# The rotary swap by transfers, two groups of query products instead of three, and the product with the values for two units in every second round

## The chip, the cores and the metric

The kernel runs on one core of a Trainium2 chip. The metric is the device time of one execution in microseconds; three runs of the kernel before were timed, and their median stands below. TensorE (PE) does the matmuls, and its weight loads are PEld. VectorE is DVE, ScalarE is ACT, GpSimd is POOL, and SyncE (SP) issues transfers.

## What is computed

The reference is one transformer block with modulated layer norms: latent attention over S = 2048 tokens with 16 heads, and then a mixture of 8 experts. The change lies in the attention:

```python
q = _rms_norm(x @ w_qa, q_a_norm_w) @ w_qb            # 96 -> 16 heads x (128 + 64)
q_nope, q_rope = (q[..., :D_NOPE], q[..., D_NOPE:])
...
x1 = x[..., ::2]                                      # _rotate_half
x2 = x[..., 1::2]
return jnp.stack((-x2, x1), axis=-1).reshape(x.shape)
...
return x * cos + _rotate_half(x) * sin                # of 64 features
...
scores = jnp.einsum('bhsd,bhtd->bhst', q_full, k_full) * scale   # causal
attn = jax.nn.softmax(scores, axis=-1)
out = jnp.einsum('bhst,bhtd->bhsd', attn, v)
```

The kernel multiplies the key's up-projection into the query, so that scores are taken between 64 latent and 64 rotary features, 128 in all, and the values are the 64 latent features.

## The kernel before

It has three stages: `prepare` (weights, layer norm, latent keys and queries), `attend`, and `experts`. The change touches the first in how the query weights are laid out, and the second.

**Units.** A pair is one head pair and one group g of 512 query tokens (PAIRS, line 54). There are 32 pairs, in the order g = 3, 1, 2, 0 within a head pair (0, 1, 2, 3 in the first). An item is one head of a pair, and a unit (line 61) is 256 keys against the 512 queries of an item: 2g full units, and two on the diagonal, of which the second needs only the last 256 queries. There are 320 units. Every item has an even number of them, so the short diagonal unit always has an odd number.

**Rounds.** All engines run through the same rounds r (line 80), each in its own order. In round r TensorE does the scores of unit r, with up to three chunks of the search for row maxima put between and behind the halves, then perhaps the broadcast of an item's shift (`shift_rows`), then perhaps one group of query products, and then the product with the values of unit r-2 (`weigh`):

```python
if part < 3:
    query_products(p, part)
if r >= 2:
    weigh(r - 2)
```

A score is three matmuls of rounded parts (high with high, high with low, low with high), upon a bank that ScalarE or VectorE has seeded with the shift. ScalarE takes the exponential of unit r and seeds the bank of unit r+2. GpSimd subtracts the 16-bit high part of the exponentials (`low_parts`, lines 664 to 676), and both parts go into the product with the values. The tiles pt and pt_lo are rings of four units.

**The query of a pair** is prepared in rounds that begin with PREP_ROUND (line 79), six rounds or more before its first chunk. Pairs 7, 11, 15, 19, 23 and 27, with g = 0, are prepared four rounds before the next pair, as pair 0 is before pair 1; else the distance is 7 to 18. From pair 2 on PREP_ROUND is even. Each of three groups of products is three matmuls of 512 columns into one of three work banks: group 0 gives head 0 (latent and rotary features), group 1 head 1, and group 2 the rotary features of both with even and odd swapped and signed. VectorE multiplies groups 0 and 1 by the cosine into qf (line 757), ScalarE copies the latent half (692), and VectorE multiplies group 2 by the sine in its bank (760) and adds it (770). Then ScalarE rounds qf to q_hi (699) and GpSimd subtracts to q_lo (661). There is one buffer qf: the next pair's first VectorE and ScalarE operations wait until q_lo of this pair is written.

**The work banks** are handed out in order by WORK_ORDER (lines 98 to 103) to chunks, shifts and query groups alike; use n waits until use n-3 has been seen by its readers (`wait_seen`).

**SyncE** loads the weights of a head pair (lines 640 to 642) once the last group of the pair before is done, and per pair four transfers of cosine and sine into turn_by (648), which has room for two pairs.

## Time and profile before

| | us |
|---|---|
| three runs | 1254.86, 1255.21, 1247.85 |
| median | 1254.86 |
| the profiled execution | 1254.86 |
| its span | 1253.1 |
| busy in the span: PE | 1146.3 (91%) |
| PEld | 958.8 (77%) |
| DVE | 846.8 (68%) |
| ACT | 787.5 (63%) |
| POOL | 690.3 (55%) |

The page gives the span in 40 slices of 31 us, each digit being tenths of a slice:

```profile
PE   2856899999999999999999999999999778989897
DVE  2632876677676776777777677776675576767676
ACT  1254577777777878777787787877777532322222
POOL 0022366777777768686787776877777711202000
PEclk9876699999999999999999999999999879989998
```

The attention is the stretch of nines. A matmul's record holds its way through the array, and the records of successive matmuls overlap; how often one starts is read from the start times in the view in order of time. Averages over the whole span mix the three stages.

### The profile page before, as it was taken

What the parts mean: (1) busy time and instruction counts of PE and PEld (TensorE: products, weight loads), DVE (VectorE), ACT (ScalarE), POOL (GpSimd) and SP (SyncE); (2) the same over time, 40 slices, a digit from 0 to 9 for tenths busy, and PEclk for the clock granted to TensorE, in tenths of its full rate; (3) what the DMA queues carried; (4) which work ended last, traced back from release to release, by engine and by line L of the source; (5) the groups of instructions that cost most, each with busy time, mean ns of one, the idle gap of its engine ahead of it and who ended that gap; (6) DMA issues with size and microseconds to landing.
All of it is one profiled execution on the core that took longest, in us unless ns stands there. A gap on an engine that the chain in (4) does not pass through costs nothing. (4 is left out here: it accounts for less than half of the span.)

```text
span 1253.1 us, 27841 instructions
## 1 busy us (share of the span) xinstructions
PE 1146.3 (91%) x11372; PEld 958.8 (77%) x11372; DVE 846.8 (68%) x1900; ACT 787.5 (63%) x1166; POOL 690.3 (55%) x569
## 2 busy tenths in 40 slices
PE   2856899999999999999999999999999778989897
PEld 1744577888888888888888888888887667888886
DVE  2632876677676776777777677776675576767676
ACT  1254577777777878777787787877777532322222
POOL 0022366777777768686787776877777711202000
PEclk9876699999999999999999999999999879989998
DMA  9301110000100200100020020010000310000000
GB/s 277 95 1 48 29 44 18 2 18 25 38 19 2 62 2 19 44 19 19 2 62 18 2 61 2 19 44 19 18 2 1 114 57 1 1 18 1 18 18 17
DMA packets 57695, 39.91 MB, mean 32 GB/s; under 512 B 7744, under 2 KB 57152, under 8 KB 57408
## 3 DMA queue, kind: packets, MB, share of 16 engines
q1 hardware_dynamic: 51216, 33.94, 9.2%
q10 hardware_dynamic: 6352, 4.19, 1.4%
q8 instruction: 90, 1.47, 0.5%
q14 instruction: 37, 0.30, 0.1%
HBM read 33.66 MB, written 4.46 MB: 30 GB/s over the span
## 5 line engine op out<-in xcount | busy, mean ns | idle before, releaser
L669 POOL TENSOR_TENSOR pt_lo<-pt 128x1024 f16<-128x1024 f32 x192 | 370.5, 1939 | 181.5 <-ACT pt L726 181.2
L782 DVE TENSOR_REDUCE gates<-bank 128x1 f32<-128x512 f32 x384 | 261.6, 689 | 148.0 <-PE bank L849 145.1
L717 ACT ACTIVATE pair<-shift 128x1024 f32<-128x1024 f32 x256 | 263.7, 1030 | 12.2 <-ACT pt L730 0.4
L726 ACT ACTIVATE pt<-pair 128x1024 f32<-128x1024 f32 x192 | 196.2, 1022 | 108.3 <-PE pair L876 107.7
L891 PEld LDWEIGHTS bank<-values,pt 128*128 128x128 bf16 x2176 | 196.8, 98 | 80.1 <-issue 52.6
L891 PE MATMUL bank<-values,pt 128*128 128x65 f16 x2176 | 235.2, 194 | 6.0 <-DVE lat L808 5.1
L893 PE MATMUL bank<-values,pt 128*128 128x64 f16 x2176 | 231.8, 192 | 0.0
L895 PE MATMUL bank<-values,pt_lo 128*128 128x65 f16 x2176 | 230.8, 194 | 0.0
L675 POOL TENSOR_TENSOR pt_lo<-pt 128x512 f16<-128x512 f32 (+3 forms) x256 | 178.3, 722 | 45.0 <-ACT pt L730 44.9
L893 PEld LDWEIGHTS bank<-values,pt 128*128 128x128 bf16 x2176 | 202.0, 98 | 0.0
L895 PEld LDWEIGHTS bank<-values,pt_lo 128*128 128x128 f16 x2176 | 201.3, 97 | 0.0
L779 DVE CUSTOM_DVE_ANT_0 bank<-bank,mask 128x128 f32<-128x128 f32 (+3 forms) x256 | 126.1, 498 | 53.8 <-PE bank L849 48.7
L730 ACT ACTIVATE pt<-pair 128x512 f32<-128x512 f32 (+3 forms) x256 | 110.4, 437 | 45.7 <-PE pair L876 32.1
L876 PE MATMUL pair<-q_hi,kt_a_hi 128*128 128x512 f32 (+1 forms) x320 | 131.1, 410 | 0.0
L876 PE MATMUL pair<-q_hi,kt_b_hi 128*128 128x512 f32 (+1 forms) x320 | 130.5, 408 | 0.0
L849 PE MATMUL bank<-kt_a_hi,q_hi 128*128 128x512 f32 (+2 forms) x320 | 118.6, 375 | 3.4 <-DVE qf L757 1.6
L849 PE MATMUL bank<-kt_b_hi,q_hi 128*128 128x512 f32 (+2 forms) x320 | 117.4, 369 | 0.7 <-DVE gates L779 0.6
L876 PE MATMUL pair<-q_lo,kt_a_hi 128*128 128x512 f32 (+1 forms) x320 | 117.2, 366 | 0.0
L876 PE MATMUL pair<-q_hi,kt_a_lo 128*128 128x512 f32 (+1 forms) x320 | 117.2, 366 | 0.0
L876 PE MATMUL pair<-q_hi,kt_b_lo 128*128 128x512 f32 (+1 forms) x320 | 117.1, 366 | 0.0
L876 PE MATMUL pair<-q_lo,kt_b_hi 128*128 128x512 f32 (+1 forms) x320 | 116.6, 364 | 0.0
L661 POOL TENSOR_TENSOR q_lo<-qf,q_hi 128x512 fp32r<-128x512 f32 x64 | 84.4, 1340 | 19.6 <-ACT q_hi L699 18.1
(218 smaller groups left out, 2380.0 us busy)
## 6 DMA issues: line engine op xcount, KB each, us to landing
turn_by<-rope_cos_by_feature SPq DMA_DIRECT2D x64, 128.0 KB, 3.0
turn_by<-rope_sin_by_feature SPq DMA_DIRECT2D x64, 128.0 KB, 3.0
xs<-in_L_attn_x ACTq DMA_DIRECT2D x1, 2048.0 KB, 25.5
lat<-in_L_attn_w_o SPq DMA_DIRECT2D x1, 2048.0 KB, 26.6
xs_again<-in_L_attn_x SPq DMA_DIRECT2D x1, 2048.0 KB, 8.1
out<-xs_again SPq DMA_DIRECT2D x4, 512.0 KB, 2.8
lat<-in_L_wmod SPq DMA_DIRECT2D x1, 1536.0 KB, 16.3
lat<-in_L_attn_w_qb SPq DMA_DIRECT2D x1, 1152.0 KB, 8.0
```

Of the source, the lines that this page charges most:

```text
L669: pool.tensor_tensor(out=pt_lo[:, at].rearrange("p a n -> p (a n)"), in0=full, in1=cut(full), op=ALU.subtract).then_inc(low_ok, 1)
L675: pool.tensor_tensor(out=pt_lo[:, at, half, live(u, half):], in0=full, in1=cut(full), op=ALU.subtract).then_inc(low_ok, 1)
L717: act.activation(s_pair[u % 2][:, :, :], shift[:, item % SHIFTS:item % SHIFTS + 1, :].to_broadcast([P, 2, BW]), ACT.Copy).then_inc(seeded[ ...
L726: act.activation(pt[:, at], s_pair[u % 2][:, :, :], ACT.Exp).then_inc(exp_done, 1)
L730: act.activation(pt[:, at, half, live(u, half):], s_pair[u % 2][:, half, live(u, half):], ACT.Exp).then_inc(exp_done, 1)
L779: dve.tensor_tensor_reduce(out=of, in0=of, in1=mask16[:, BW - n * P:], scale=1.0, scalar=LOWEST, op0=ALU.add, op1=ALU.max, accum_out=to).t ...
L782: dve.tensor_reduce(out=to, in_=of, axis=AXX, op=ALU.max).then_inc(work_seen["v"], 1)
L849: pe.matmul(work_of(w)[:, 0:cols], q, kt_hi[h][:, part * BW:part * BW + cols], start=True, stop=True).then_inc(work_done, 1)
L876: last = pe.matmul(to, keys[a], q[b], start=False, stop=(m == 2), skip_group_check=True)
L891: pe.matmul(to, cut(pt[:, at, half, mine]), with_one, start=(u == FIRST_UNIT[item] and half == 0 and t == 0), stop=False, skip_group_check ...
L893: pe.matmul(to[:, 0:KVL], cut(pt[:, at, half, mine]), low_values, start=False, stop=False, skip_group_check=True)
L895: last = pe.matmul(to, pt_lo[:, at, half, mine], with_one, start=False, stop=end, skip_group_check=True)
```

## The change

- In `prepare` the rotary columns of the query weights are laid out as evens and then odds (32 + 32), and the third block is no longer built; the keys' rotary features get the same order.
- A pair has two groups of products: group 0 gives the rotary features of both heads, group 1 the latent features of both.
- VectorE reads group 0 with three operations: by_sin = product x sign x sine, and the two products with the cosine into qf. Four transfers issued by SyncE then copy by_sin, its halves of 32 rows exchanged, into a new tile, swapped. Before a pair's four, SyncE issues the next pair's loads, with the tables in eight transfers instead of four.
- GpSimd adds swapped to qf in the third round of the preparation, after that round's low parts. ScalarE copies both latent halves in the second round. q_hi and q_lo come in the fourth round instead of the third.
- `weigh` is called for units r-3 and r-2 in odd rounds, and not in even ones.

```diff
-    WORK_ORDER += [("q", *PREP_AT[_r])] if _r in PREP_AT and PREP_AT[_r][1] < 3 else []
+    WORK_ORDER += [("q", *PREP_AT[_r])] if _r in PREP_AT and PREP_AT[_r][1] < 2 else []
 WORK = {w: n for n, w in enumerate(WORK_ORDER)}
 
 
 def seen_by(n):
 
     use = WORK_ORDER[n]
-    return {"max": "v", "shift": "a", "q": "va"}[use[0]] if use[0] != "q" or use[2] < 2 else ""
-
-
-SEEN = {e: [0, *itertools.accumulate(e in seen_by(n) for n in range(len(WORK_ORDER)))] for e in "av"}
+    return {"max": {"v": 1}, "shift": {"a": 1}, "q": {"v": 3} if use[-1] == 0 else {"a": 2}}[use[0]]
+
+
+SEEN = {e: [0, *itertools.accumulate(seen_by(n).get(e, 0) for n in range(len(WORK_ORDER)))] for e in "av"}
+
+
+def values_due(r):
+
+    return (r - 3, r - 2) if r >= 3 and r % 2 else ()
...
-                for at, e, of, sgn in moves:
-                    act.activation(pair_cols(wq_hi, at, e), of, ACT.Copy, scale=sgn).then_inc(wqh_ok, 1)
+                for at, of in moves:
+                    act.activation(half_cols(wq_hi, at), of, ACT.Copy).then_inc(wqh_ok, 1)
...
-                weights_of = None
-                weights_in = 0
-                for p, (hp, g) in enumerate(PAIRS):
-                    if hp != weights_of:
-                        weights_of, weights_in = hp, weights_in + 1
+                def loads(p):
+                    hp, g = PAIRS[p]
+                    if p == 0 or hp != PAIRS[p - 1][0]:
                         if p > 0:
-                            sp.wait_ge(work_done, WORK[("q", p - 1, 2)] + 1)
+                            sp.wait_ge(work_done, WORK[("q", p - 1, 1)] + 1)
                         for part in range(2):
                             sp.dma_start(wq[part][:, :].bitcast(F32), wq_dram[part, hp]).then_inc(wq_in, 16)
                     if p > 1:
-                        sp.wait_ge(q_sum, 2 * p - 2)
+                        wait_seen(sp, WORK[("q", p - 2, 0)])
                     for n, name in enumerate(("cos_t", "sin_t")):
-                        of = k[name].rearrange("d (j g p) -> d j g p", j=BT, g=NG)[:, :, g, :]
+                        of = k[name].rearrange("(i e) (j g p) -> e i j g p", e=2, j=BT, g=NG)[:, :, :, g, :]
                         for half in range(2):
-                            sp.dma_start(turn_by[half * DR:half * DR + DR, p % 2, n, :].rearrange("d (j p) -> d j p", j=BT),
-                                         of).then_inc(turn_in[p % 2], 16)
-                sp.wait_ge(wq_in, 32 * weights_in)
+                            for e in range(2):
+                                at = half * DR + e * (DR // 2)
+                                sp.dma_start(turn_by[at:at + DR // 2, p % 2, n, :].rearrange("d (j p) -> d j p", j=BT),
+                                             of[(e + n) % 2]).then_inc(turn_in[p % 2], 16)
+
+                def swap(p):
+                    wait_seen(sp, WORK[("q", p, 0)])
+                    if p > 0:
+                        sp.wait_ge(q_sum, 2 * p)
+                    for at in range(0, P, DR // 2):
+                        sp.dma_start(swapped[at:at + DR // 2, :], by_sin[at ^ (DR // 2):(at ^ (DR // 2)) + DR // 2, :]).then_inc(q_swapped, 16)
+
+                loads(0)
+                for p in range(len(PAIRS)):
+                    if p + 1 < len(PAIRS):
+                        loads(p + 1)
+                    swap(p)
+                sp.wait_ge(q_swapped, 64 * len(PAIRS))
+                sp.wait_ge(wq_in, 32 * NP)
                 for n in range(2):
-                    sp.wait_ge(turn_in[n], 64 * (len(PAIRS) // 2))
+                    sp.wait_ge(turn_in[n], 128 * (len(PAIRS) // 2))
 
             @block.gpsimd
             def _(pool):
                 pool.memset(ones_r[:, :].bitcast(F32), 1.0).then_inc(consts_ok, 1)
+
+                def query_sum(p, r):
+                    if r >= 0:
+                        pool.wait_ge(low_ok, OPS[r + 1])
+                    pool.wait_ge(q_swapped, 64 * p + 64)
+                    for hd in range(2):
+                        pool.tensor_tensor(out=qf[ROT[hd], hd, :], in0=swapped[ROT[hd], :], in1=qf[ROT[hd], hd, :],
+                                           op=ALU.add).then_inc(q_sum, 1)
+                        pool.wait_ge(q_sum, 2 * p + hd + 1)
 
                 def query_low(p):
                     for hd in range(2):
...
                 for r in ROUNDS:
                     if 0 <= r < NU:
                         low_parts(r)
-                    p, part = PREP_AT.get(r, (0, 3))
+                    p, part = PREP_AT.get(r, (0, 4))
                     if part == 2:
+                        query_sum(p, r)
+                    if part == 3:
                         query_low(p)
...
-                def query_plain(p, part):
-                    n = WORK[("q", p, part)]
-                    if part == 0 and p > 0:
+                def query_plain(p):
+                    n = WORK[("q", p, 1)]
+                    if p > 0:
                         act.wait_ge(q_lo_ok, 2 * p)
                     act.wait_ge(work_done, n + 1)
-                    act.activation(qf[PLAIN[part], part, :], work_of(n)[PLAIN[part], :], ACT.Copy).then_inc(work_seen["a"], 1)
+                    for hd in range(2):
+                        act.activation(qf[PLAIN[hd], hd, :], work_of(n)[PLAIN[hd], :], ACT.Copy).then_inc(work_seen["a"], 1)
 
                 def query_high(p):
                     if p >= Q_SLOTS:
                         act.wait_ge(s_done, 2 * FIRST_UNIT[2 * (p - Q_SLOTS) + 2])
+                    wait_seen(act, WORK[("q", p, 1)])
+                    act.wait_ge(q_sum, 2 * p + 2)
                     for hd in range(2):
-                        act.wait_ge(q_sum, 2 * p + hd + 1)
                         act.activation(q_hi[:, p % Q_SLOTS, hd, :], qf[:, hd, :], ACT.Copy).then_inc(q_hi_ok, 1)
...
-                def query_turn(p, part):
-                    n = WORK[("q", p, part)]
-                    if part == 0:
-                        if p > 0:
-                            dve.wait_ge(q_lo_ok, 2 * p)
-                        dve.wait_ge(turn_in[p % 2], 64 * (p // 2 + 1))
+                def query_turn(p):
+                    n = WORK[("q", p, 0)]
+                    if p > 0:
+                        dve.wait_ge(q_lo_ok, 2 * p)
+                        dve.wait_ge(q_swapped, 64 * p)
+                    else:
+                        dve.wait_ge(sign_ok, 3)
+                    dve.wait_ge(turn_in[p % 2], 128 * (p // 2 + 1))
                     dve.wait_ge(work_done, n + 1)
-                    if part < 2:
-                        rot = ROT[part]
-                        dve.tensor_tensor(out=qf[rot, part, :], in0=work_of(n)[rot, :], in1=turn_by[rot, p % 2, 0, :],
+                    dve.scalar_tensor_tensor(out=by_sin[:, :], in0=work_of(n)[:, :], scalar=sign[:, :], in1=turn_by[:, p % 2, 1, :],
+                                             op0=ALU.mult, op1=ALU.mult).then_inc(work_seen["v"], 1)
+                    for hd in range(2):
+                        dve.tensor_tensor(out=qf[ROT[hd], hd, :], in0=work_of(n)[ROT[hd], :], in1=turn_by[ROT[hd], p % 2, 0, :],
                                           op=ALU.mult).then_inc(work_seen["v"], 1)
-                    else:
-                        dve.tensor_tensor(out=work_of(n)[:, :], in0=work_of(n)[:, :], in1=turn_by[:, p % 2, 1, :],
-                                          op=ALU.mult).then_inc(q_turned, 1)
-                        query_sum(p)
-
-                def query_sum(p):
-                    for part in range(2):
-                        wait_seen(dve, WORK[("q", p, part)])
-                    dve.wait_ge(q_turned, p + 1)
-                    by_sin = work_of(WORK[("q", p, 2)])
-                    for hd in range(2):
-                        dve.tensor_tensor(out=qf[ROT[hd], hd, :], in0=by_sin[ROT[hd], :], in1=qf[ROT[hd], hd, :],
-                                          op=ALU.add).then_inc(q_sum, 1)
...
-                    if r >= 2 and UNITS[r - 2][2] == 2:
-                        evacuate(r - 2)
+                    for u in values_due(r):
+                        if UNITS[u][2] == 2:
+                            evacuate(u)
...
-                    if part < 3:
+                    if part < 2:
                         query_products(p, part)
-                    if r >= 2:
-                        weigh(r - 2)
+                    for u in values_due(r):
+                        weigh(u)
```

## Rows read from the trace of the kernel before

**Rows 1.** The page: its first line.

```profile
span 1253.1 us, 27841 instructions
```

**Rows 2.** Busy by stretch: PE, PEld, DVE, ACT, POOL (count), granted clock, DMA share, GB/s.

```profile
160.00:950.00 790.00, 787.73 (x9055) 648.35 (x9055) 567.85 (x1198) 623.79 (x825) 584.67 (x471) 1.00 0.08 23
```

**Rows 3.** In order of time, TensorE, behind a product with the values: start, us, what.

```profile
602.01 0.47 PE L876 MATMUL pair<-q_hi,kt_b_hi 128*128 128x512 f32 x1
602.33 0.39 PE L876 MATMUL pair<-q_lo,kt_b_hi 128*128 128x512 f32 x1
602.55 0.40 PE L876 MATMUL pair<-q_hi,kt_b_lo 128*128 128x512 f32 x1
```

**Rows 4.** In order of time, TensorE, rounds 58 and 59: group 0 to group 1.

```profile
301.82 0.40 PE L837 MATMUL bank<-ql_hi,wq_pair_hi 96*128 96x512 f32 x1
...
302.53 0.21 PE L891 MATMUL bank<-values,pt 128*128 128x65 f16 x1
...
303.27 0.27 PE L867 MATMUL pair<-ident,mask 128*128 128x128 bf16 x2
...
304.49 0.39 PE L837 MATMUL bank<-ql_hi,wq_pair_hi 96*128 96x512 f32 x1
```

**Rows 5.** VectorE in order of time; the last is a group: busy us, mean ns.

```profile
302.83 0.69 DVE L757 TENSOR_TENSOR qf<-bank,turn_by 64x512 f32<-64x512 f32 x1
...
125.47 1.41 DVE L757 TENSOR_TENSOR qf<-bank,turn_by 64x512 f32<-64x512 f32 x2 [2.56 <-POOL q_lo L661]
126.80 0.68 DVE L760 TENSOR_TENSOR bank<-bank,turn_by 128x512 f32<-128x512 f32 x1
...
L442 DVE SCALAR_TENSOR_TENSOR gates<-gates,junk 128x512 f32<-128x512 f32 x1 | 0.7, 691 | 0.0
```

**Rows 6.** In order of time, TensorE, rounds 62 and 63 (preparation of pair 8).

```profile
314.06 0.21 PE L891 MATMUL bank<-values,pt 128*128 128x65 f16 x1
...
314.81 0.27 PE L867 MATMUL pair<-ident,mask 128*128 128x128 bf16 x2
...
316.16 0.40 PE L837 MATMUL bank<-ql_hi,wq_pair_hi 96*128 96x512 f32 x1
```

**Rows 7.** In order of time, GpSimd, round 60: unit 60, then pair 7.

```profile
309.00 1.90 POOL L669 TENSOR_TENSOR pt_lo<-pt 128x1024 f16<-128x1024 f32 x1 [3.50 <-ACT pt L726]
310.98 2.54 POOL L661 TENSOR_TENSOR q_lo<-qf,q_hi 128x512 fp32r<-128x512 f32 x2
```

**Rows 8.** SyncE's issues in order of time; then transfers: count, KB, us to landing.

```profile
308.64 0.31 SPq L642 DMA_DIRECT2D wq_pair_hi<-wq_parts  x1
...
309.47 1.19 SPq L648 DMA_DIRECT2D turn_by<-rope_cos_by_feature  x2
...
turn_by<-rope_sin_by_feature SPq DMA_DIRECT2D x64, 128.0 KB, 3.0
...
wq_pair_hi<-wq_parts SPq DMA_DIRECT2D x8, 144.0 KB, 2.2
```

**Rows 9.** In order of time: q_hi of pair 1, TensorE's first chunk on it.

```profile
128.34 1.35 ACT L699 ACTIVATE q_hi<-qf 128x512 fp32r<-128x512 f32 x2 [1.67 <-DVE qf L770]
...
133.01 0.89 PE L849 MATMUL bank<-kt_a_hi,q_hi 128*128 128x512 f32 x2
```

**Rows 10.** End of the stage: TensorE in order of time, and two stretches.

```profile
973.01 0.20 PE L891 MATMUL bank<-values,pt 128*128 128x65 f16 x1 [1.80 <-DVE lat L808]
...
993.84 1.97 PE L1306 MATMUL bank<-ident,lat_n 128*128 128x128 f32 x8 [3.73 <-POOL lat_n L1043]
997.75 0.47 PE L1306 MATMUL bank<-ident,lat_n 128*128 128x128 f32 x1 [1.94 <-POOL lat_n L1043]
...
992.00:993.00 1.00, 0.00 (x0) 0.00 (x0) 1.00 (x2) 0.80 (x1) 1.00 (x1) 0.69 0.78 114
990.00:1005.00 15.00, 9.33 (x56) 8.82 (x53) 8.84 (x12) 5.95 (x8) 9.95 (x7) 0.66 0.93 299
```

**Rows 11.** In order of time, VectorE behind the preparation of the query weights.

```profile
43.88 0.17 DVE L426 COPY modc<-bank 128x8 f32<-128x8 f32 x1 [1.60 <-PE bank L518]
```

More of the change, by code:

```diff
@@ L584, in attend @@
     with ExitStack() as own:
[L585 removed]
+        wq = [sb(own, f"wq_pair_{p}", [QL, 2 * P], F32R) for p in ("hi", "lo")]
         turn_by = sb(own, "turn_by", [P, 2, 2, BW])
@@ L589, in attend @@
         qf = sb(own, "qf", [P, 2, BW])
+        by_sin = sb(own, "by_sin", [P, BW])
+        swapped = sb(own, "swapped", [P, BW])
+        sign = sb(own, "sign", [P, 1])
         pt = sb(own, "pt", [P, PT_RING, 2, BW])
```

58 lines of the change are left out of this document (27 added, 31 removed).

## Prediction

> **What bounds the kernel now.** I read the page first, then the busy time by stretches, then the instructions in order of time. The profiled execution took 1254.86 us, which is the median of the three runs; its span is 1253.1 us [rows 1]. All changes below are added to 1254.9. From 160 to 950 us TensorE is busy for 787.7 of 790 us at the full clock, while VectorE has 568, ScalarE 624 and GpSimd 585 [rows 2]. This is the attention stage, 320 rounds. So here a matmul taken away shortens the kernel by its issue interval, and a wait put in lengthens it by its whole length. The other engines have 20 to 28% of free time, but each has its own order, and the change rearranges those orders.
>
> One trap: a 512-column matmul is shown with 0.39 to 0.40 us, but the next starts 0.22 to 0.23 us later [rows 3]; the rest is overlap. Intervals count, not durations.
>
> **What is taken from TensorE.** The third group of query products goes: three matmuls per pair. The three of a group take 301.82 to 302.53 = 0.71 us [rows 4]. Pairs 0 and 1 are prepared before TensorE is the bound, so 30 x 0.71 = **-21.3 us**. By durations it would be 36, and wrong.
>
> The products with the values come in every second round, so half of the 320 changes from them back to scores go. After such a change the first score matmul is followed after 0.32 us (602.01 to 602.33), else after 0.22 to 0.23 [rows 3]: 0.09 us. Units whose scores begin with the 16-bit mask matmuls pay it anyhow; of the 160 odd units 64 are such. 96 x 0.09 = **-8.6 us**. The bounds are 0, if the weights' load is not hidden in the new place either, and 160 x 0.09 = 14.
>
> **What no longer fits: the bank of the first group.** The three work banks go round. In an even round R the order is chunk, chunk, query group 0; in R+1 it is chunk, chunk, group 1, so group 1 takes the bank of group 0. Now group 0 is released by VectorE only after three operations instead of one, and no product with values lies between, since R is even for every pair from 2 on. VectorE started its first operation 302.83 - 301.82 = 1.01 us after group 0's first matmul began [rows 4, 5]. Three such operations took 125.47 to 127.48 = 2.01 us [rows 5]; the added multiplication by a sign is bounded by the one scalar_tensor_tensor of that shape, 691 ns, the same price [rows 5]. TensorE's own work from there to group 1 is 0.71 + (304.49 - 303.27 = 1.22) = 1.93 us [rows 4], because the unit in R+1 is a short one (256 columns) for pairs 3 to 28. Wait: 3.02 - 1.93 = 1.1 us; where the chunks are full, 314.81 to 316.16 = 1.35 [rows 6], it is 0.95. I take 1.05. Pairs 8, 12, ... 28 fall under the next part, 20 are left: **+21 us**. Pairs 29 to 31 have a full unit there (8 matmuls of 0.23 = 1.84 us): 3 x 0.4 = **+1.3**.
>
> **The low parts of the queries.** VectorE may not begin pair p+1 before GpSimd has written q_lo of pair p. Pairs 7, 11, 15, 19, 23 and 27 (group 0 of their head pair) are prepared only 4 rounds before the next. Before, q_lo of pair 7 ended at 313.52 and VectorE wanted it at about 314.1: the end of that pair's group 0, some 0.6 us later [rows 6, 7]. Now q_lo comes a round later on GpSimd, behind one more unit's low part, and two additions are put ahead of both. On the axis of before: GpSimd starts the low part of unit 60 at 309.00; then 1.90 for it, 2.54 for the additions (unknown, taken as the two subtractions of q_lo, which also read and write 4-byte values), 1.90 for unit 61, 2.54 for q_lo [rows 7], 2.01 for VectorE's three: 319.9. TensorE stood before group 1 of pair 8 at 316.16; 0.71 (the dropped group, after unit 60's scores) and 0.75 (unit 60's product with the values, 314.06 to 314.81) are gone from before it, and a change of 0.1: 314.6 [rows 6]. Wait 5.3 us. If an addition costs half of the 1024-column subtraction, 0.95 us [rows 7], it is 4.7.
>
> The swap is on this chain too. SyncE first waits for pair 7's group 1, issues two weight loads (308.64 to 309.47) and then pair 8's tables, eight transfers where four took 0.6 us each [rows 8], and only then the four swap transfers. Half the rows each: 0.31 to 0.62 us, 2.5 to 5 in all; the swaps at most 0.31 each; landing 2.2 to 3.0 [rows 8]. The trace has no transfer inside SBUF; the nearest are these. Pair 7's group 1, whose last result came 0.9 us after 304.49, is done at about 304.6 on this axis, since 0.74 us of products with the values (302.53 to 303.27) move behind it [rows 4]. This gives 310.5 to 314.6, against GpSimd ready at 310.9. Nearest to the low end (96 rows were issued in 0.31 us, so issue time seems to go with the rows): 0.3 us late. So 5.6 us, 4.7 to 9; six times: **+34 us**. In the other pairs the swap has four microseconds more and is hidden.
>
> **Start.** For pairs 0 and 1 nothing covers the chain from VectorE over the swap, the additions and q_hi to q_lo, on which the next pair's turning waits. Each loop gains the swap (0.6 + 2.4) and GpSimd's additions (2.54) and loses VectorE's (two of 64 x 512: 1.41 [rows 5]): 4.1. q_hi of pair 1 ended at 129.7; 8.2 more is 137.9. Its first chunk ran at 133.01 [rows 9]. **+5 us** (3.6 with cheap additions; 8 if the sixteen table loads that stand before the first swap take 0.62 each).
>
> **The clock.** At the end of the stage TensorE stopped at 990.1 and took up again at 993.84. The granted clock, 1.00 before, has a mean of 0.69 in 992:993: it fell to 0.50 (1.2 GHz) at 992.4. The mean of 990:1005 is 0.66, so it stayed there for some 10.2 us, to 1002.6, although work without a gap began at 997.75 [rows 10]. So it fell after 2.3 us of idleness and came back after 4.9 us of work, which loses 2.4 us. An idleness of 1.8 us at 973.01 [rows 10] left it at 1.00. The waits of 5.6 us are of the first kind, those of 1.1 of the second: 6 x 2.4 = **+14 us**, bounds 0 and 20. The Trainium skill (TensorE: Matmul & The Clock Gate, "HAM oscillation") says that one long wait in each loop makes every following batch start at half rate. By that rule the sum holds with this term; without it, it would be 14 us less, a case below.
>
> **GpSimd's two lumps in other pairs.** The additions and q_lo put 5.1 us into two rounds. Two full rounds leave GpSimd 2 x (1.84 + 0.74 - 1.90) = 1.4 us [rows 4, 7], and unit 60's low part (ended 310.9) was used at 314.06, 3.1 us later [rows 6, 7]. Short by 0.6 us, by the cheaper additions not at all: 14 pairs with full units behind them, 0 to 10 us, I take **+4**. ScalarE's q_hi, which now waits for GpSimd, lies in the same wait.
>
> **Priced at nothing:** VectorE's dropped additions (44 us of busy time, no bound); the shorter weight preparation (behind its pieces VectorE idles 1.6 us for TensorE until 43.88 [rows 11]); half the value products being a round later, since the pt ring of four was sized for u-4 and both are done before round u's exponentials; the experts.
>
> **Sum:** 1254.9 - 21.3 - 8.6 + 21 + 1.3 + 34 + 5 + 14 + 4 = **1304 us**, 3.9% slower.
>
> **Rivals.**
> 1. *The waits are covered* (VectorE frees the bank in time, GpSimd runs ahead): only the start is left, 1254.9 - 29.9 + 5 = 1230. For it: 20 to 28% of free time on every helper, and hardly a wait in the trace. Against it: both waits are in each engine's order, whatever its load. It needs three operations in under 1.5 us. Chance 0.13.
> 2. *The clock holds*, and additions and swap are at their cheap ends: 1304 - 14 - 4 - 6 = 1280, to 1290 with central prices. For it: one long idleness alone is in the trace at that level. Chance 0.22.
> 3. *The long wait is halved* (additions on 64 partitions at half price, short bank wait 0.5 us): 1254.9 - 29.9 + 11 + 15 + 5 = 1256, no difference. Chance 0.08.
> 4. *The swap's transfers are slow*, each loop landing at the late end: waits of 9 us, +20, some 1324. Chance 0.07, beyond the range in half of it.
>
> The forecast has 0.50. The case that decides the sign is the wait for q_lo: the gain of 30 us is used up when the waits sum to 30, which is six of 5.0 alone, or 28 of 1.05.
>
> **How the numbers follow.** The range leaves out about 1 in 10 below (most of rival 1) and 1 in 10 above: 1240 to 1324; the likeliest case's own is 1290 to 1320. Faster by over 1% (below 1242; 1% is about what this kernel's measurement tells from no change) 0.13, within 1% 0.08, slower 0.79.
>
> **What would show it.** Right: group 1's products waiting some 1 us for VectorE's turning in about 20 pairs; six waits of over 4.5 us behind q_lo, with the granted clock below 1.00 right after them; a first pair-1 chunk near 138; score matmuls after a round without values at 0.23 us. Wrong: TensorE still busy for 99.7% of the stage, or the swap's transfers landing after more than 4 us, or GpSimd's additions far from 1.27 us each.

## The result, and the profile after

| | us |
|---|---|
| before, median of 4 runs | 1254.6 (1247.85 to 1255.21) |
| after, median of 4 runs | 1372.22 (1370.29 to 1375.36) |
| ratio | 1.095, 95% interval 1.092 to 1.098 |
| forecast | 1304, range 1240 to 1324 |

The change makes the kernel slower by 117.6 us. The direction was forecast; the size was 49, and the result lies outside the range.

**Where in the span.** The page's first line, against [rows 1]:

```profile
span 1370.5 us, 27902 instructions
```

Two stretches of the attention stage, each about a head pair and each from one fall of the clock, inside a long wait, to the next, against [rows 2] (columns as there). From the first query product of a head pair to that of the next it took 105.7 us before; now it takes 123.2 in the mean of five (122.8 to 123.9). TensorE is busy for about as long as before (105.6), although four groups of products are gone, and the granted clock is no longer 1.00:

```profile
341.86:464.74 122.88, 107.02 (x1200) 88.14 (x1200) 75.25 (x156) 79.87 (x109) 87.47 (x71) 0.96 0.11 28
464.74:587.62 122.88, 106.13 (x1200) 87.45 (x1200) 75.23 (x156) 81.87 (x112) 89.24 (x72) 0.96 0.11 28
```

**What TensorE waits for**, in the view of waits of TensorE, whole run (us in total, times, longest). These five are new; before, there were 0.3 us of the second and nothing of the others:

```profile
PE bank L860 <- DVE qf L788: 78.3, 29, 9.9
PE bank L914 <- POOL pt_lo L693: 30.1, 43, 3.8
...
PE bank L872 <- ACT q_hi L727: 8.9, 2, 5.8
...
PE pair L899 <- ACT pair L745: 7.1, 15, 1.8
...
PE pair L890 <- ACT pair L745: 2.9, 8, 0.4
```

L860 is a group of query products; VectorE's qf at L788 is the last of the three operations that release group 0's bank. L914 is the product with the values, which needs GpSimd's low part (L693). L899 and L890 are scores, which need ScalarE's seed (L745).

The same view of the second of those stretches alone. The four rows add up to 17.8 us (a wait that a stretch cuts is counted whole):

```profile
PE bank L860 <- DVE qf L788: 13.2, 4, 9.9
PE bank L914 <- POOL pt_lo L693: 3.5, 6, 0.9
PE pair L899 <- ACT pair L745: 0.7, 2, 0.4
PE pair L890 <- ACT pair L745: 0.4, 1, 0.4
```

That head pair, from the start of its long wait at 461.46 to the start of the next at 585.37, takes 123.9 us, 18.2 longer than before. 17.8 of waits and 1.8 for half speed (below), less 2.84 for four dropped groups and 1.1 for twelve changes from values to scores, give 15.7. The missing 2.5 us lie at the waits themselves, in two parts that the rows don't show. A wait is listed from the end of the record before it, and that record outlasts the moment at which the next matmul would have started by some 0.16 us: the wait listed with 9.90 us is 10.30 from start to start, where 0.23 is usual. Thirteen waits make 2.1. And a 512-column matmul behind a wait is followed after 0.34 instead of 0.23 us; behind the waits before the values nothing of the kind is seen.

**The long wait in order of time.** The preparation of pairs 11 and 12, which stand to one another as 7 and 8 do, TensorE first (start, us, what, idle before and releaser). The first line is the short wait, the second the long one:

```profile
450.33 0.50 PE L860 MATMUL bank<-ql_hi,wq_pair_hi 96*128 96x512 f32 x1 [1.13 <-DVE qf L788]
471.36 0.79 PE L860 MATMUL bank<-ql_hi,wq_pair_hi 96*128 96x512 f32 x1 [9.90 <-DVE qf L788]
```

GpSimd in the same stretch, against [rows 7]: low part of unit 100, the two additions of pair 11, low part, q_lo. (The prediction's working was for unit 60 and pair 7. Of the six places this one has the longest wait; in the other five the additions waited for the swap for 3.27 to 3.69 us.)

```profile
455.67 1.89 POOL L693 TENSOR_TENSOR pt_lo<-pt 128x1024 f16<-128x1024 f32 x1 [5.65 <-ACT pt L754]
462.08 2.59 POOL L678 TENSOR_TENSOR qf<-swapped,qf 64x512 f32<-64x512 f32 x2 [4.51 <-DMA swapped<-by_sin]
464.75 1.89 POOL L693 TENSOR_TENSOR pt_lo<-pt 128x1024 f16<-128x1024 f32 x1
466.60 2.49 POOL L685 TENSOR_TENSOR q_lo<-qf,q_hi 128x512 fp32r<-128x512 f32 x2
```

GpSimd stood idle for 4.51 us in front of the additions, with a low part and q_lo queued behind them. What it waited for is in SyncE's row, against [rows 8]: two weight loads, eight tables, and only then the four swap transfers:

```profile
451.33 0.33 SPq L641 DMA_DIRECT2D wq_pair_hi<-wq_parts  x1
451.70 0.43 SPq L641 DMA_DIRECT2D wq_pair_lo<-wq_parts  x1
452.17 1.85 SPq L649 DMA_DIRECT2D turn_by<-rope_cos_by_feature  x4
454.07 1.87 SPq L649 DMA_DIRECT2D turn_by<-rope_sin_by_feature  x4
456.04 2.43 SPq L657 DMA_DIRECT2D swapped<-by_sin  x4
```

and in the answer on the swap's line for 450 to 466 us, which gives the four transfers' time from issue to landing:

```profile
DMA to landing us min/median/max: 1.9/2.0/4.1
```

The fourth began at 457.88 and landed 4.1 us later, when the additions start. That is the slowest of all 128 swap transfers; in the other five places the fourth landed after 2.0 to 3.0 us. On VectorE the next turning waits for q_lo, against [rows 5]:

```profile
469.12 0.75 DVE L785 SCALAR_TENSOR_TENSOR by_sin<-bank,sign,turn_by 128x512 f32<-128x512 f32 x1 [8.98 <-POOL q_lo L685]
469.90 1.41 DVE L788 TENSOR_TENSOR qf<-bank,turn_by 64x512 f32<-64x512 f32 x2
```

From the additions' start to the bank's release are 9.3 us, foretold with 9.0. The chain's links were priced rightly; its start was not.

**The clock behind it**, four stretches against [rows 10]: 0.50 until 475, while work is on from 471.36.

```profile
460.00:465.00 5.00, 1.46 (x11) 1.09 (x10) 0.14 (x1) 0.22 (x1) 2.77 (x3) 0.97 0.34 93
465.00:470.00 5.00, 0.00 (x0) 0.00 (x0) 0.85 (x2) 4.32 (x8) 5.00 (x4) 0.50 0.01 3
470.00:475.00 5.00, 3.64 (x43) 3.02 (x44) 2.54 (x5) 1.18 (x2) 1.79 (x4) 0.50 0.22 52
475.00:480.00 5.00, 5.00 (x61) 4.20 (x58) 2.47 (x10) 2.86 (x3) 1.79 (x1) 1.00 0.41 107
```

**The start**, against [rows 9]: the first swap stands behind sixteen tables (115.68 to 123.23), and pair 1's first chunk runs at 142.87, not at 133.01.

```profile
123.27 2.49 SPq L657 DMA_DIRECT2D swapped<-by_sin  x4
...
142.87 0.98 PE L872 MATMUL bank<-kt_a_hi,q_hi 128*128 128x512 f32 x2 [3.05 <-ACT q_hi L727]
```

**Changes from values to scores**, against [rows 3]: after the chunk that ends a round without values the scores follow one another after 0.23 us, and the interval of 0.32 is gone there.

```profile
454.43 0.40 PE L899 MATMUL pair<-q_hi,kt_b_hi 128*128 128x512 f32 x1
454.66 0.40 PE L899 MATMUL pair<-q_lo,kt_b_hi 128*128 128x512 f32 x1
```

The attention ends 123.0 us later (the last product with the values starts at 1112.92 instead of 989.92). The experts' stage, where nothing was changed, is 5.6 us shorter.

### The profile page after: what moved, and what is told of

It reads as the page before. It is cut to its first block and busy times, and to the rows that moved or that the text cites. A ratio compares the mean times of both kernels' runs of the same rounds, so it can differ in the third digit from the quotient of the medians.

```text
span 1370.5 us, 27902 instructions
## 1 busy us (share of the span) xinstructions
PE 1139.5 (83%) x11276; PEld 955.2 (70%) x11276; DVE 824.7 (60%) x1835; ACT 768.3 (56%) x1162; POOL 776.1 (57%) x633
## 5 line engine op out<-in xcount | busy, mean ns | idle before, releaser
L693 POOL TENSOR_TENSOR pt_lo<-pt 128x1024 f16<-128x1024 f32 x192 | 367.2, 1924 | 194.8 <-ACT pt L754 189.5
L745 ACT ACTIVATE pair<-shift 128x1024 f32<-128x1024 f32 x256 | 263.4, 1029 | 11.9
L914 PE MATMUL bank<-values,pt 128*128 128x65 f16 x2176 | 228.2, 196 | 30.7 <-POOL pt_lo L693 30.1
L914 PEld LDWEIGHTS bank<-values,pt 128*128 128x128 bf16 x2176 | 200.9, 100 | 72.5 <-POOL pt_lo L693 36.8
L916 PE MATMUL bank<-values,pt 128*128 128x64 f16 x2176 | 225.8, 195 | 0.0
L918 PE MATMUL bank<-values,pt_lo 128*128 128x65 f16 x2176 | 225.0, 197 | 0.0
L916 PEld LDWEIGHTS bank<-values,pt 128*128 128x128 bf16 x2176 | 204.2, 99 | 0.0
L699 POOL TENSOR_TENSOR pt_lo<-pt 128x512 f16<-128x512 f32 (+3 forms) x256 | 181.2, 734 | 37.2 <-ACT pt L758 37.0
L758 ACT ACTIVATE pt<-pair 128x512 f32<-128x512 f32 (+3 forms) x256 | 104.1, 431 | 62.6 <-PE pair L899 57.2
L899 PE MATMUL pair<-q_hi,kt_a_hi 128*128 128x512 f32 (+1 forms) x320 | 128.8, 402 | 4.3 <-ACT pair L745 4.3
L899 PE MATMUL pair<-q_hi,kt_b_hi 128*128 128x512 f32 (+1 forms) x320 | 127.4, 398 | 2.8 <-ACT pair L745 2.8
L899 PE MATMUL pair<-q_hi,kt_a_lo 128*128 128x512 f32 (+1 forms) x320 | 118.2, 369 | 0.0
L899 PE MATMUL pair<-q_lo,kt_a_hi 128*128 128x512 f32 (+1 forms) x320 | 117.7, 368 | 0.0
L899 PE MATMUL pair<-q_hi,kt_b_lo 128*128 128x512 f32 (+1 forms) x320 | 117.2, 366 | 0.0
L899 PE MATMUL pair<-q_lo,kt_b_hi 128*128 128x512 f32 (+1 forms) x320 | 116.7, 365 | 0.0
L678 POOL TENSOR_TENSOR qf<-swapped,qf 64x512 f32<-64x512 f32 x64 | 84.6, 1322 | 48.3 <-DMA swapped<-by_sin 43.9
```

The costliest lines, as they stand in the source:

```text
L693: pool.tensor_tensor(out=pt_lo[:, at].rearrange("p a n -> p (a n)"), in0=full, in1=cut(full), op=ALU.subtract).then_inc(low_ok, 1)
L699: pool.tensor_tensor(out=pt_lo[:, at, half, live(u, half):], in0=full, in1=cut(full), op=ALU.subtract).then_inc(low_ok, 1)
L745: act.activation(s_pair[u % 2][:, :, :], shift[:, item % SHIFTS:item % SHIFTS + 1, :].to_broadcast([P, 2, BW]), ACT.Copy).then_inc(seeded[ ...
L758: act.activation(pt[:, at, half, live(u, half):], s_pair[u % 2][:, half, live(u, half):], ACT.Exp).then_inc(exp_done, 1)
L899: last = pe.matmul(to, keys[a], q[b], start=False, stop=(m == 2), skip_group_check=True)
L914: pe.matmul(to, cut(pt[:, at, half, mine]), with_one, start=(u == FIRST_UNIT[item] and half == 0 and t == 0), stop=False, skip_group_check ...
```

## The experiments

My theory after the comparison: the loss is made of (a) the short wait for group 0's bank, (b) the q_lo chain through the one buffer qf, made longer by swaps that stand behind tables, (c) GpSimd's additions as a lump in front of low parts, (d) the start, (e) the clock after the long wait. Rivals: the grouping of the values is what costs; transfers cost by themselves; GpSimd is simply full.

The kernel before was timed anew beside each group of runs: 1254.49, 1254.28 and 1255.07 us. The experts' stage, which no edit touches, takes 257 to 265 us in the profiled runs, by where its clock falls. That is as much as some of the effects below, so the end of the attention (the start of the last product with the values, in the profiled run) is given beside the time. It is 1112.92 in the changed kernel.

| run | median us | ratio to before, 95% |
|---|---|---|
| e1 values in every round | 1380.23 | 1.099 (1.096 to 1.102) |
| e2 before, values in pairs | 1261.67 | 1.006 (1.004 to 1.008) |
| e3 swap first | 1352.61 | 1.078 (1.077 to 1.080) |
| e4 one round earlier | 1325.84 | 1.056 (1.054 to 1.058) |
| e5 second qf | 1331.78 | 1.063 (1.061 to 1.065) |
| e6 sums on VectorE | 1323.71 | 1.056 (1.054 to 1.059) |
| e7 three repairs | 1265.61 | 1.009 (1.008 to 1.011) |
| e8 four repairs | 1258.87 | 1.006 (1.003 to 1.008) |
| e9 e8, values in every round | 1286.67 | 1.023 (1.021 to 1.026) |
| e10 e9, group 1 later | 1293.28 | 1.031 (1.029 to 1.032) |
| e11 e7, values in every round | 1289.06 | 1.028 (1.026 to 1.030) |

### e1: the values in every round again

```diff
 def values_due(r):
-    return (r - 3, r - 2) if r >= 3 and r % 2 else ()
+    return (r - 2,) if r >= 2 else ()
```

> The changed kernel with the values of unit r-2 in every round again; everything else of the change stays. My theory: the grouping itself is a gain of 96 x 0.09 = 8.6 us, which goes, but group 0 and group 1 of the query products again have a product with the values between them (about 2.8 us), so the 1.13 us wait for group 0's bank goes in some 20 pairs (-22 us) and the long wait behind q_lo of 9.9 us is shorter by up to 2.8 us in six pairs (-17 us). 1372 + 9 - 22 - 17 = 1342 us, 1330 to 1362. Rival, the grouping is what costs (it starves ScalarE and GpSimd in short rounds): all of the 117 us but the transfers' own share goes, 1300 us or less. Rival, the transfers and GpSimd alone cost: 1372 + 9 = 1381 us, and TensorE's waits at group 1 stay as they are.

Measured 1380.2, 8 us above the changed kernel. My expectation failed by a wrong price: a unit's product with the values is 24 matmuls of 0.03 us, 0.74 us in all, not 2.8. By that it covers 0.7 us of each wait, and so it did: the short waits fell from 1.13, 1.13 and 1.02 us to 0.42, 0.52 and 0.29, the long ones to 8.2 to 9.0. But the waits for low parts grew from 30.1 to 37.8 us, and 9.4 us of waits for VectorE's copy of finished outputs (L826) came up. The time is that of the rival "transfers and GpSimd alone cost" (1381), though not by its reason, since the waits at group 1 did change. The attention ends 7.6 us later than in the changed kernel. The profiled run is 13.3 us longer; the other 5.7 lie in the experts' stage, untouched by the edit: from 1125 to 1250 us the granted clock is 0.86 against 0.93.

### e2: the grouping alone, on the kernel before

The same function put into the kernel before, in reverse of e1, for VectorE's copies and TensorE's products with the values.

> The kernel before with the values done for two units in every second round, and nothing else of the change. My theory: no interval of 0.32 us between values and scores in 96 rounds, -8.6 us, and no new wait, since group 0's bank is free after one VectorE operation of 0.7 to 0.9 us instead of three: 1246 us, 1242 to 1252. Rival, the grouping is what costs: at or above 1262 us, with waits of TensorE at the values (for GpSimd's low parts) or at the scores (for ScalarE's seeds).

Measured 1261.7: 7 us slower, where the prediction has -8.6, and about what the rival says. The head pair takes 108.5 us, not 105.7, and the attention ends 12.2 us later than before; the experts' stage is 3.5 us shorter. The gain is there: the changes from values to scores give back 0.9 us in a head pair. Over it lie new waits of TensorE, here for ScalarE's seeds (L722 in that kernel):

```profile
PE pair L882 <- ACT pair L722: 8.2, 20, 0.6
```

A round without values has 1.9 us of TensorE's work (six score matmuls and two chunks, 8 x 0.23), and ScalarE has an exponential and a seed of 1.02 + 1.03 = 2.05 us in each, plus a shift (0.6), a latent copy (0.6) or q_hi (1.3) in some. A round with values of its own took 2.6 us and hid that. "Busy for 624 of 790 us" did not say that ScalarE had no room in a round of 1.9 us.

### e3: the swap ahead of the tables

```diff
+                    swap(p)
                     if p + 1 < len(PAIRS):
                         loads(p + 1)
-                    swap(p)
```

> The changed kernel with one thing moved: SyncE issues the four swap transfers of a pair ahead of the eight table transfers of the next pair. My theory: in the six pairs with the long wait GpSimd's additions waited 4.51 us for the swap, of which 3.8 us was the issue of the tables (8 x 0.46). The long wait falls from 9.9 to about 6.1 us, 6 x 3.8 = -23 us, and pair 0's swap is issued 3.7 us earlier: 1372 - 27 = 1345 us, 1335 to 1355. Rival, the transfer itself is what is slow (its landing): the swap starts earlier but lands as late, 1365 us or more. Rival, GpSimd's own work is what sets the chain: under 6 us of gain.

Measured 1352.6, -19.6 us. The attention ends 26.5 us earlier, as expected (27), and the experts' stage is 6.9 us longer. The transfer was late because of where it stood in SyncE's queue. All six long waits are now the same, and they are the 5.6 us of the prediction:

```profile
457.15 0.80 PE L860 MATMUL bank<-ql_hi,wq_pair_hi 96*128 96x512 f32 x1 [5.53 <-DVE qf L788]
```

and GpSimd does its additions directly behind the low part:

```profile
445.83 1.89 POOL L693 TENSOR_TENSOR pt_lo<-pt 128x1024 f16<-128x1024 f32 x1 [5.65 <-ACT pt L754]
447.81 2.65 POOL L678 TENSOR_TENSOR qf<-swapped,qf 64x512 f32<-64x512 f32 x2
```

The waits at group 1 fell by 78.3 - 57.3 = 21.0 us. (The 4.51 us of the expectation were those of one place; the six long waits fell by 3.1 to 4.4.)

### e4: the preparation one round earlier

```diff
-AHEAD, PREP_AHEAD = 5, 6
+AHEAD, PREP_AHEAD = 5, 7
```

> The changed kernel with the preparation of each pair a round earlier (7 rounds ahead instead of 6), so that from pair 2 on group 0 lies at the end of an odd round, with two products with the values (5.6 us) behind it, and group 1 in the even round behind. Same work, same waits in the code. My theory: TensorE no longer reaches group 1 before VectorE's three operations on group 0's bank are done: 20 x 1.1 = -22 us, and the long wait falls from 9.9 to about 4.3 us in six pairs, -34 us, with some of the 11 us at the half clock back: 1372 - 56 = 1316 us, 1300 to 1330. Rival, GpSimd's load is what costs (its additions and the low parts): the waits move to the values and the total stays within 10 us of 1372. Rival, the grouping or the transfers cost in themselves: no change above 5 us.

Measured 1325.8, -46.4 of the expected -56. Two units' products with the values now lie between group 0 and group 1, 1.5 us and not the 5.6 of the expectation, and the short waits are gone. The waits for low parts fell from 30.1 to 2.9 us, and those for seeds rose from 10.0 to over 15. The long wait did not fall to 4.3 us but came in two pieces, first at a chunk, then at group 1:

```profile
564.62 0.80 PE L872 MATMUL bank<-kt_b_hi,q_hi 128*128 128x512 f32 x1 [4.99 <-ACT shift L734]
568.61 0.80 PE L860 MATMUL bank<-ql_hi,wq_pair_hi 96*128 96x512 f32 x1 [3.20 <-DVE qf L788]
```

The first is ScalarE's queue, which I had not followed: q_hi waits 5.60 us for GpSimd's additions, and the reading of the shift, which frees a work bank, stands behind it.

```profile
562.02 1.15 ACT L727 ACTIVATE q_hi<-qf 128x512 fp32r<-128x512 f32 x2 [5.60 <-POOL qf L678]
563.07 1.00 ACT L754 ACTIVATE pt<-pair 128x1024 f32<-128x1024 f32 x1
563.98 0.59 ACT L734 ACTIVATE shift<-bank 128x512 f32<-128x512 f32 x1
```

### e5: a second buffer qf

```diff
-        qf = sb(own, "qf", [P, 2, BW])
-        by_sin = sb(own, "by_sin", [P, BW])
+        qf = sb(own, "qf", [P, 2, 2, BW])
...
-                    if p > 0:
-                        dve.wait_ge(q_lo_ok, 2 * p)
+                    if p > 1:
+                        dve.wait_ge(q_lo_ok, 2 * p - 2)
...
-                    dve.scalar_tensor_tensor(out=by_sin[:, :], in0=work_of(n)[:, :], scalar=sign[:, :], in1=turn_by[:, p % 2, 1, :],
+                    dve.scalar_tensor_tensor(out=turn_by[:, p % 2, 1, :], in0=work_of(n)[:, :], scalar=sign[:, :], in1=turn_by[:, p % 2, 1, :],
```

> The changed kernel with two buffers qf in turn instead of one, so that a pair's turn by VectorE no longer waits for q_lo of the pair before. (Room for it: the product with the sine is written over the sine table in its slot, and the shifts have three slots instead of four.) The transfers, GpSimd's work and the values two by two stay. My theory: the six long waits of 8.7 to 9.9 us fall to the 1.1 us of every other pair, 6 x 8.5 = -51 us, and with them goes the half clock behind them, some -11 us: 1372 - 62 = 1310 us, 1300 to 1325. Rival, GpSimd is simply full there: the chain comes back one step on (ScalarE behind q_hi, the chunks' banks, the values behind the low parts), and less than 25 us are gained. Rival, the clock falls in any case: 1321 us.

Measured 1331.8, -40.4 of -62. The first half holds: no wait at group 1 is over 1.8 us, and they sum to 30.7 instead of 78.3. The rest is the rival's step: GpSimd is still late for the swap, and the low part behind its additions is late for the values. The waits for low parts rose from 30.1 to 38.0 us, with one of 0.8 to 2.1 us where the long wait had been:

```profile
570.83 0.50 PE L861 MATMUL bank<-ql_hi,wq_pair_hi 96*128 96x512 f32 x1 [1.02 <-DVE qf L789]
574.11 0.23 PE L915 MATMUL bank<-values,pt 128*128 128x65 f16 x1 [1.56 <-POOL pt_lo L695]
```

### e6: the additions on VectorE

```diff
-                    if part == 2:
-                        query_sum(p, r)
...
                     if part == 0:
                         query_turn(p)
+                    if part == 2:
+                        query_sum(p)
```

The first place is GpSimd's, the second VectorE's.

> The changed kernel with the two additions of the swapped rows done by VectorE instead of GpSimd, in the same rounds. My theory: GpSimd's 2.6 us lump in front of its next low part goes, and with it most of TensorE's waits at the values (30 us) and some of the waits for ScalarE (4 us); the chain in front of the long wait is shorter by 2.6 - 1.4 = 1.2 us in six pairs: 1372 - 30 - 7 = 1335 us, 1322 to 1350. Rival, what GpSimd was waiting for costs as much in VectorE's queue: VectorE stands up to 4.5 us before the swap with chunk maxima and item shifts behind it, TensorE waits for banks instead, and the time stays within 10 us of 1372.

Measured 1323.7, -48.5, more than expected. TensorE's waits for low parts fell from 30.1 to 0.3 us and those for ScalarE's seeds from 10.0 to 0.4: in the changed kernel both come from GpSimd's lump. (With e1's edit, without the grouping, the seeds keep 9.3.) The rival's mechanism is there as well, in six places: VectorE waits for the late swap (5.82 us in the first row below) with chunk maxima behind it, and TensorE waits there for 3.5 to 4.8 us. That took the place of the long wait and is half its size.

```profile
561.46 1.40 DVE L784 TENSOR_TENSOR qf<-swapped,qf 64x512 f32<-64x512 f32 x2 [5.82 <-DMA swapped<-by_sin]
```

```profile
563.51 0.44 PE L870 MATMUL bank<-kt_b_hi,q_hi 128*128 128x384 f32 x1 [4.52 <-DVE gates L796]
```

### e7 and e8: the repairs together

e7 is e3, e4 and e5 at once; e8 is e7 with e6.

> Three repairs on the changed kernel at once: swap transfers ahead of the tables, preparation one round earlier (7), two buffers qf. Alone the first gave -19.6 us and the second -46.4 us; with the second, what stayed of the long wait were 3.9 to 5.3 us for ScalarE (its reading of the shift stands behind q_hi, which waits for GpSimd's sum) and 3.19 us for the turn. My theory: the 3.19 us go with the second qf, most of the 3.9 to 5.3 us with the earlier swap, the half clock with both: 1326 - 6 x 7.2 - 10 - 4 = 1269 us, 1258 to 1285. Rival, the transfers or the additions themselves cost: above 1300 us.

> The three repairs, and the additions on VectorE as well. My theory: with the preparation in odd rounds GpSimd's lump was covered (TensorE's waits for low parts fell from 30 to 3 us in that run), so moving the additions gains little: within 6 us of the run with three repairs, 1255 to 1275. Rival, GpSimd's load is the cause: at least 15 us faster than the run with three repairs.

Measured 1265.6 and 1258.9. 107 and 113 of the 118 us are gone, and the attention ends at 999.93 and 993.35, against 989.92 before the change. In a head pair of e7 all of TensorE's waits come to 2.9 us, and the clock is 1.00:

```profile
525.90:632.60 106.70, 103.80 (x1201) 85.86 (x1201) 76.72 (x157) 81.86 (x113) 90.08 (x73) 1.00 0.13 34
```

With the swap early and the rounds odd, GpSimd's additions cost 7 us (e7 against e8; 6.6 by the end of the attention), at the edge of the 6 expected, and not the 30 to 49 of the changed kernel. e8's head pair is 105.8 us in the mean of five, as long as the 105.7 before the change: the 108.5 us of e2 less 4 x 0.71 for the dropped groups is 105.7. So a head pair of e8 is as long as the two parts of the change that act on TensorE make it, at their measured prices. What is left of TensorE's waits in it is the grouping's: waits for ScalarE's seeds are 15.7 us in e7 and 11.0 in e8, as they were 8.2 in e2. The median of e8 is 4.6 us above that of the kernel before (ratio 1.006), and 3.4 of these are there when the attention ends. They come from the start, where pair 4 is prepared 4.5 us later.

### e9, e10, e11: without the grouping

e9 is e8 with e1's edit, e10 is e9 with group 1 issued behind its round's values, e11 is e7 with e1's edit.

> The kernel with four repairs, with the values of one unit in every round again, as in the kernel before. What stays of the change are the swap by transfers and the two groups of query products. My theory: the grouping costs 2.96 us in each of the periods of four pairs (108.44 against 105.48 us when it was put alone on the kernel before) and with four repairs the period is 105.5 us, which is that of the kernel before, less three... four dropped groups x 0.71, plus those 2.96. Without it: -23 us; but group 1 lies only one unit's values and scores behind group 0 and waits 0.3 to 0.5 us for its bank in three pairs of four, +9 us: 1259 - 23 + 9 = 1245 us, 1236 to 1252. Rival, the grouping is a gain in this setting, as read in the trace of before (-8.6): 1259 + 9 + 9 = 1277 us. Rival, the transfers still cost something of their own that hides: no change within 5 us.

> The same kernel as the run with four repairs and the values in every round, with group 1 of the query products issued behind the values of its round instead of ahead of them: 0.74 us later, so that VectorE's three operations on group 0's bank are done. My theory: the waits of 0.3 to 0.5 us go, -7 us against that run: 1238 us, 1230 to 1246. Rival, what is late moves on to ScalarE's copy of the latent half and q_hi: no gain.

> Three repairs (GpSimd adds) with the values in every round. My theory: with the values of unit r-2 due in round r GpSimd's 2.6 us lump is no longer covered by a round's delay, so TensorE waits for low parts again, some 4 to 5 us in each period of four pairs: against the same kernel with the additions on VectorE (1245 us expected) +30 us: 1275 us, 1260 to 1290. Rival, GpSimd's additions never cost anything once the swap comes in time: within 5 us of the run with four repairs and the values in every round.

Measured 1286.7, 1293.3 and 1289.1. e9 and e10 are misses, and in the other direction: without the grouping e8 loses 28 us instead of gaining 14. e11 lies within its range (1260 to 1290), and in part for its reason: against e7 it is 23.5 us slower, and the waits for low parts rose from 5.0 to 19.4 us, half of what was expected. What all three expectations missed is a wait at the values for VectorE's copy of the output, 21.7 us in e9 (first row). In e11 it is 9.5 us, beside the waits for low parts (second row):

```profile
PE bank L911 <- DVE lat L821: 21.7, 17, 5.1
```

```profile
PE bank L915 <- POOL pt_lo L695: 19.4, 23, 2.1
```

So e9 and e11 take the same time by different waits. That GpSimd's additions cost nothing, as e11's rival has it, doesn't follow: VectorE pays for them in e9, GpSimd in e11.

With the values in every round the copy of a finished item must be made before the next round's values. In e9 VectorE has the additions in front of it, and they wait for the swap (VectorE of e9; TensorE's next product with the values, at 484.38, waited 1.57 us for this copy):

```profile
482.58 1.40 DVE L783 TENSOR_TENSOR qf<-swapped,qf 64x512 f32<-64x512 f32 x2 [1.34 <-DMA swapped<-turn_by]
483.90 0.41 DVE L821 COPY lat<-bank 128x260 f32<-128x260 f32 x1
```

With the grouping, an item's last unit is of an odd number, the next product with the values comes two rounds later, and the copy has a round more. e10 shows the same from the other side: moving group 1 behind the values removed nearly all waits at group 1 (11.4 to 1.9 us) and put them, and more, before the values (21.7 to 42.2). So the grouping costs 7 us where helpers are in time (e2), and is worth 8 in the changed kernel (e1), 23.5 in e7 (e11) and 28 in e8 (e9). It has no one price: it makes rounds too short for ScalarE (waits for seeds of 15.7 and 11.0 us in e7 and e8, of 0.7 and none without it in e11 and e9) and gives GpSimd and VectorE a round more. The waits of e9 do not add up to all of the 28; the rest, with the clock (0.97 in two head pairs of e9), is not taken apart.

No version here beats the kernel before.

## Why the prediction was right in direction and wrong in size

**Dropped groups, -21.3: nothing speaks against it.** e8's head pair bears it out (105.7 worked out from e2 with it, 105.8 measured); no run dropped the groups alone.

**Changes from values to scores, -8.6: right as an interval, and not the whole price.** The interval went as read, 0.9 us in a head pair, and in the changed kernel it costs 8 us to undo the grouping (e1). But the prediction priced the grouping only on TensorE. By itself (e2) it costs 7 us: ScalarE's 2.05 us do not fit into a round of 1.9. "20 to 28% of free time" was an average over rounds, and the change made the rounds unequal.

**Short waits, 20 x 1.05 + 3 x 0.4 = +22: right.** Measured 19 of 1.02 to 1.14 (some 21 us) and 0.58, 0.50 and 0.52 for pairs 29 to 31. e4 removed them by 2 units of values between the groups, which confirms the reason.

**Long waits, 6 x 5.6 = +34: the mechanism was right, the size wrong.** Six waits, 9.90, 9.08, 8.96, 8.85, 8.71 and 8.67, 54.2 us. The term that failed is "0.3 us late" for the swap: the additions waited for it for 3.3 to 4.5 us, 3.6 in the mean. The prediction had bounds for each part and chose the low end by the rule that issue time goes with the rows. It does not: a table of 32 rows in four pieces took 0.46 us and more (3.9 to 5.1 for eight, not 2.5), and a swap transfer of 32 rows 0.60 (2.4 or more, not 1.2); the last one landed after 2.0 to 4.1 us, foretold with 2.2. From the first table's issue to that landing it was 8.5 to 9.8 us, where the low ends make 5.9: 2.6 to 3.9 us more, which with the 0.3 is the lateness within half a microsecond. The high ends were in the text (5 us of tables, a wait of 9) and got a chance of 0.07 as rival 4. With the swap out of the way (e3) the wait is 5.53, so the other links together were right.

**Clock, 6 x 2.4 = +14: about right.** After the long wait that ends at 471.36 work ran for 3.6 us at 0.50, which loses 1.8 us; in the other five places it was 3.4 to 5.6 us, some 12 us lost in six. The Trainium skill (TensorE: Matmul & The Clock Gate, "HAM oscillation") says that a long wait in every loop makes each next batch start at half rate; this trace agrees, six times of six, at 0.96 for the stretches shown, and 1.00 in the head pair of e7 shown above, where the waits are gone. Rival 2 is out. A seventh fall, at 191.67, stands at a wait of 3.80 us for a low part, behind a seventh late swap, and costs 1.7. A surprise stands in the last section.

**GpSimd's two lumps, +4: failed.** TensorE's new waits for low parts and for seeds are 30 + 10 us. The additions took 1.32 us each, near the 1.27 foretold, so the price was right and the slack was not. The prediction set 5.1 us against the spare time of two equal rounds of 2.6 us, and drew the bound of 10 from that alone. With the values in pairs it matters where the lump lies. Additions in an even round delay the low part of the odd unit behind them, which is used two rounds after its scores; an even unit's is used three rounds after. e4, whose additions lie in odd rounds, has 2.9 us of waits for low parts; e11, with odd rounds but the values in every round, has 19.4. e6, without the additions on GpSimd, has 0.3, with 0.4 for seeds.

**Start, +5: too small.** 9.9 us at pair 1's first chunk, 12.0 at the first score (153.77 against 141.77). Bounded by 8 for slow table loads; the swap's own issue (2.4 for 1.2) and 1.3 us in the stage before came on top.

**Priced at nothing.** VectorE's dropped additions and the value products' round gave no wait; the round even took one away, 5.1 us for VectorE's copy of finished outputs in the kernel before. That a wait costs more than the row says was not priced either. The experts, with 5.6 us less than before, were not foreseen; the edit does not touch them.

**The sum.** In the profiled runs the miss is 117.4 - 49.3 = 68 us. Long waits +20.6, low parts and seeds +36, start +7, clock 0 and experts -5.6 make 58. From 160 us on there are some 84 more waits than before, whose two parts that no row shows (0.16 us at each, 0.11 at some 44 with a 512-column matmul behind) come to some 18 us, and 5 us of old waits are gone: 71, with estimates in it of a few microseconds each.

**In the range.** Even with the prediction's own high ends (long waits of 9, +20; start 8, +3; lumps 10, +6; clock 20, +6) it would have been 1339. The long waits are no more than that. What put the result beyond it is the lump, 40 us against a bound of 10 that was drawn from equal rounds, and after it the 18 us at the waits that no row shows.

## What to carry to other kernels

Moving an operation from a free engine to a transfer puts its result behind everything on the issuing queue and behind every in-order engine that waits for it: follow the wait through SyncE, GpSimd, ScalarE and VectorE, and list what each has queued behind it, before any of it is priced at nothing. Issue the transfer that somebody waits for ahead of those that are for later. Compare a helper's work with the shortest round, not with the average, once a change makes the rounds unequal.

## What the runs showed of the hardware

- A transfer's issue time on SyncE did not go with its rows: 96 rows of 1 KB 0.33 to 0.43 us, 32 rows in four pieces of 512 bytes 0.46, 32 rows of 2 KB inside SBUF 0.60. Half of the 128 swap transfers landed within 2.0 us of their issue and all but one within 3.3; the one took 4.1.
- The clock fell without a long wait too. In e5 the nearest waits are of 1.02 and 1.56 us, 3.3 us apart; it fell to 0.50 during the second, at 573.67, and its mean from 575 to 578 is 0.65:

```profile
569.00:572.00 3.00, 1.98 (x20) 1.28 (x20) 2.94 (x6) 0.00 (x0) 2.46 (x2) 1.00 0.28 72
572.00:575.00 3.00, 1.44 (x36) 1.31 (x32) 0.04 (x1) 2.71 (x5) 2.92 (x3) 0.78 0.49 131
575.00:578.00 3.00, 3.00 (x21) 2.58 (x19) 0.36 (x2) 2.93 (x6) 3.00 (x4) 0.65 0.26 65
```

  That happened at three of the six places of e5 where the long wait had been, with a second wait of 1.31 to 2.07 us; at the other three it was 0.81 to 1.20 us and the clock stayed at 1.00. In the prediction a single wait of 1.8 us had left it at 1.00 [rows 10]. The Trainium skill (TensorE: Matmul & The Clock Gate, "A second HAM failure mode: psum-queue depth-cycling") describes falls from frequent short idle times in each iteration; this trace has them in half of its head pairs, so it agrees in part.
- An addition of 64 x 512 four-byte values on GpSimd takes 1.28 us in the median, as long as a subtraction of 128 x 512 (2.49 for two): half the partitions did not halve it. On VectorE the same addition took 0.7 (e6).
